# Routing of tokens inside an attention loop: fewer VectorE instructions, cut into short pieces, and a new schedule of the row scatters

## The reference, cut to what matters

```python
logits = jnp.einsum('btd,ed->bte', x, w_router)
probs = jax.nn.softmax(logits, axis=-1)
vals, idx = jax.lax.top_k(probs, TOP_K)
gates = jnp.sum(jax.nn.one_hot(idx, N_EXPERTS, dtype=x.dtype) * vals[..., None], axis=-2)
...
acc = acc + jnp.einsum('bted,bte->btd', y, gates)
```

## Time and profile before

| | |
|---|---|
| median of three runs | 961.9 us (958.61 to 963.03) |
| the profiled execution | 967.59 us, of which the span is 965.8 us |
| attention ends, on VectorE's last write of x | 486.3 us |
| TensorE busy in the span | 86% |
| mean granted TensorE clock | 0.919 of full speed |

### The profile page before, as it was taken

One profiled execution on the slowest core, in us unless ns is written; L12 is line 12 of the kernel. 1 busy time (PEld: TensorE's weight loads), 2 busy tenths in 40 slices (PEclk: granted clock), 3 DMA queues, 4 the chain that ended last, 5 costly groups with the idle time before them and its releaser, 6 DMA issues.

```text
span 965.8 us, 14197 instructions
## 1 busy us (share of the span) xinstructions
PE 832.7 (86%) x4630; PEld 454.8 (47%) x4630; DVE 731.3 (76%) x1571; ACT 633.4 (66%) x1119; POOL 469.4 (49%) x778
## 2 busy tenths in 40 slices
PE   5699999999988988798788799999974747899996
PEld 4123322223222222222176577877763425678884
DVE  6787888888898868983368588887767866787873
ACT  2157888888876777668467477776653682666773
POOL 3715273737355664536465048876576607411211
PEclk9569999999999989989679899999995877999999
DMA  7735546464636354303012346666616000000001
GB/s 243 164 113 164 125 147 143 141 149 136 153 125 156 98 170 87 146 16 112 20 63 101 116 165 225 249 214 216 210 58 235 17 17 1 1 0 13 12 22 44
DMA packets 45477, 110.72 MB, mean 115 GB/s; under 512 B 7886, under 2 KB 20814, under 8 KB 40086
## 3 DMA queue, kind: packets, MB, share of 16 engines
q1 hardware_dynamic: 39245, 97.86, 33.6%
q0 software_dynamic: 4992, 10.36, 3.1%
q10 hardware_dynamic: 1167, 1.60, 0.5%
HBM read 57.58 MB, written 51.03 MB: 112 GB/s over the span
## 4 chain that ended last, share of the span: by engine, by line
PE 48%; DVE 21%; ACT 10%; issue 9%; POOL 8%; DMA 3%; SPq 1%; another core or an unknown queue 0%; POOLq 0%; DVEq 0%; ACTq 0%
PE PS L1087 10%; DVE mx L895 9%; PE PS L1076 7%; PE PS L1057 4%; POOL yd L1303 4%; PE PS L320 3%; PE PS L322 3%; PE PS L321 3%; ACT E L801 3%; DMA HT<-xs 2%; PE PS L1039 2%; PE PS L1024 1%; DVE cb L2341 1%; ACT ov L807 1%; PE PS L2444 1%
## 5 line engine op out<-in xcount | busy, mean ns | idle before, releaser
L895 DVE TENSOR_REDUCE mx<-PS 128x2 f32<-128x1024 f32 x256 | 305.8, 1220 | 66.9 <-PE PS L1057 62.8
L801 ACT ACTIVATE E<-PS 128x512 f32<-128x512 f32 x512 | 274.3, 599 | 68.2 <-PE PS L1076 65.1
L1076 PE MATMUL PS<-Q,K 51*128 51x512 bf16 x512 | 168.0, 401 | 14.8 <-ACT E L801 10.6
L1057 PE MATMUL PS<-K,Q 48*128 48x512 bf16 x512 | 142.1, 411 | 27.5 <-DVE mx L895 26.6
L1087 PE MATMUL PS<-E,V 128*9 128x512 f32 x1024 | 142.0, 629 | 0.0
L1303 POOL DMA_INDIRECT yd<-yt,goes x92 | 99.4, 1080 | 45.9 <-issue 24.7
L1076 PEld LDWEIGHTS PS<-Q,K 51*128 51x128 bf16 x512 | 37.6, 95 | 165.7 <-ACT E L801 95.7
L1470 DVE TENSOR_TENSOR Gl<-Gf,Gh 128x512 fp32r<-128x512 f32 x117 | 84.6, 739 | 26.1 <-ACT Gh L1338 19.9
L513 POOL DMA_INDIRECT xs<-HT,pos x64 | 64.0, 1000 | 79.5 <-ACT E L801 45.6
L1332 ACT ACTIVATE Gf<-PS,WR 128x512 f32<-128x512 f32 x92 | 63.3, 689 | 42.6 <-PE PS L322 34.0
L2341 DVE SCALAR_TENSOR_TENSOR cb<-ye,gt,cb 128x128 f32<-128x128 f32 x224 | 60.3, 344 | 0.0
(11 more groups left out here) (418 smaller groups left out, 1854.9 us busy)
## 6 DMA issues: line engine op xcount, KB each, us to landing
WR<-wsd SPq DMA_DIRECT2D x23, 1028.0 KB
xs<-zero SPq DMA_DIRECT2D x8, 2112.0 KB, 7.3
wsd<-wsp SPq DMA_DIRECT2D x8, 1024.0 KB, 4.1
HT<-xs SPq DMA_DIRECT2D x23, 264.0 KB
dqk<-SPL SPq DMA_DIRECT2D x30, 192.0 KB, 2.8
Q<-dqk SPq DMA_DIRECT2D x14, 384.0 KB, 5.5
K<-dqk SPq DMA_DIRECT2D x14, 384.0 KB
stage<-in_w SPq DMA_DIRECT2D x9, 516.0 KB
```

The costliest lines, as they stand in the source:

```text
L801: e.activation(E[:, m % 4, n % 4], PS[:, bank["exp", n], :], ACT.Exp).then_inc(*k.inc("exp", n))
L895: e.tensor_reduce(mx[:, 2 * s % 96:2 * s % 96 + 2], PS[:, o:o + 2, :], AX.X, ALU.max, negate=True).then_inc(*k.inc("max", s))
L1057: return e.matmul(PS[:, o + n % 2, :], Q[r, b % 3, h // 2, qt * P:(qt + 1) * P], K[r, b % 3, h // 2, :], start=True, stop=True)
L1076: e.matmul(PS[:, o, :], K[r, b % 3, h // 2, kt * P:(kt + 1) * P], Q[r, b % 3, h // 2, :], start=True, stop=True).then_inc(*k.inc("exp_mm", n))
```

## The change

It fuses or drops ten VectorE instructions of each group of the routing (36 become 26): the copy of the best expert's index (`dve_one_hot` writes it to its place), the masking of the best before the second (one instruction for two), one copy in the gates, five of the starts (a masked scan, whose first column carries the count of the group before, replaces the corrections after it), and in the places the two multiplications and the two reductions become one of each, of double width. It cuts the parts into eleven pieces of two to four instructions, and moves them: group 0's best to batch 3 at i = 52 and 60, the rest to batch 4 at i = 4, 12, 22, 28, 34, 44, 48, 52, 60; group 1 likewise in batches 5 and 6; group 2 in batch 7 to i = 38, 48 and 54; group 3 in `ffn0` to (1, 3), (2, 1) and (2, 2), with `tiles_of` at (2, 3) in place of (3, 2). ScalarE's and TensorE's parts move with them; in `ffn0` `act_exp` goes from (2, 1) to (2, 0) and the ranks from (2, 2) to (2, 0). On GpSimd `wsplit` and `max_parts(b+1, 0)` go ahead of the scatters at 36. Two tiles more go in batch 7 at unit 58, tiles 22 and 23 behind the last product with V, and tiles 24 to 31 in `ffn0` without waits for gelus. On SyncE the load of the weights of tile 9 and of a pack of 1005 KB (`p2`) go behind the first three row loads. The core of the diff:

```diff
+        def dve_rest(e, k, M, wk):
+            k.wait_own("v")
+            e.scalar_tensor_tensor(wk[:, 3], wk[:, 0], -3.0e38, M, ALU.mult, ALU.add).then_inc(*k.inc("v"))
+            k.wait_own("v")
...
-            e.tensor_scalar(wk[:, 3], wk[:, 0], -3.0e38, None, ALU.mult).then_inc(*k.inc("v"))
-            k.wait_own("v")
-            e.tensor_tensor(wk[:, 3], wk[:, 3], M, ALU.add).then_inc(*k.inc("v"))
...
+        def dve_best_a(e, k, g):
             L, w, a, c = group(g)
             k.wait_ge("lgt", c // 4 - 1)
-            dve_top1(e, k, L, w)
-            k.wait_own("v")
-            e.tensor_copy(HT[:, a:c, 129], w[:, 4, :, 2])
+            dve_equal(e, k, L, w[:, 4, :, 0], w[:, 2])
+            dve_ordered(e, k, w[:, 2])
+
+        def dve_best_b(e, k, g):
+            L, w, a, c = group(g)
+            dve_one_hot(e, k, w[:, 2], HT[:, a:c, 129], w[:, 0])
+
+        def dve_second_a(e, k, g):
+            L, w, a, c = group(g)
+            dve_rest(e, k, L, w)
+            dve_equal(e, k, w[:, 3], w[:, 4, :, 1], w[:, 2])
+
+        def dve_second_b(e, k, g):
+            L, w, a, c = group(g)
+            dve_ordered(e, k, w[:, 2])
+            dve_one_hot(e, k, w[:, 2], w[:, 4, :, 2], w[:, 1])
...
-            chain(k, e.reciprocal(w[:, 4, :, 4], w[:, 4, :, 5]))
-            chain(k, e.tensor_tensor(w[:, 4, :, 5], w[:, 4, :, 3], w[:, 4, :, 4], ALU.mult))
-            e.tensor_copy(HT[:, a:c, 130], w[:, 4, :, 5])
-            e.tensor_tensor(HT[:, a:c, 131], w[:, 4, :, 4], w[:, 4, :, 5], ALU.subtract).then_inc(*k.inc("gates", g))
+            e.reciprocal(w[:, 4, :, 4], w[:, 4, :, 5]).then_inc(*k.inc("v"))
+
+        def dve_gates_b(e, k, g):
+
+            L, w, a, c = group(g)
+            k.wait_own("v")
+            chain(k, e.tensor_tensor(HT[:, a:c, 130], w[:, 4, :, 3], w[:, 4, :, 4], ALU.mult))
+            e.tensor_tensor(HT[:, a:c, 131], w[:, 4, :, 4], HT[:, a:c, 130], ALU.subtract).then_inc(*k.inc("gates", g))
...
-            chain(k, e.tensor_tensor_scan(inc, one[:, 0:8 * n], tot, 0.0, ALU.mult, ALU.add))
-            chain(k, e.tensor_copy(e8[:, 0, 1:8], over[:, 0:7, n - 1]))
-            e.tensor_tensor(cnt, over[:, :, n - 1], zero_, ALU.subtract)
-            chain(k, e.tensor_tensor(bs, base, zero_, ALU.subtract))
-            e.tensor_tensor(base, base, cnt, ALU.add)
-            chain(k, e.tensor_tensor(inc, inc, tot, ALU.subtract))
-            e.tensor_tensor(over, over, bs.unsqueeze(2).to_broadcast([P, 8, n]), ALU.add).then_inc(*k.inc("v"))
+            chain(k, e.tensor_tensor_scan(inc, mask(n), tot, 0.0, ALU.mult, ALU.add))
+            if g < 3:
+                e.tensor_copy(by_expert(starts(g + 1)[1])[:, :, 0], by_expert(inc)[:, :, n]).then_inc(*k.inc("v"))
...
-            for x in range(2):
-                chain(k, e.tensor_tensor(w[:, x], w[:, x], w[:, 3], ALU.mult))
-                chain(k, e.tensor_reduce(posf[:, x, a:c], w[:, x], AX.X, ALU.add))
+            e.tensor_tensor(w[:, 0:2], w[:, 0:2], w[:, 3:4].to_broadcast([P, 2, n, 8]), ALU.mult).then_inc(*k.inc("v"))
...
+            chain(k, e.tensor_reduce(posf[:, :, a:c], w[:, 0:2], AX.X, ALU.add))
...
@@ pool of attention: the loop over batches, and behind it
+                    wsplit(b + 1)
+                    if b + 1 < NB:
+                        max_parts(b + 1, 0)
                     if b >= 5:
                         paced(b, 36, SENT[b] + 4, SENT[b] + 6)
-                    wsplit(b + 1)
                     if b == 7:
                         paced(b, 48, SENT[b] + 6, SENT[b] + 8)
-                    if b + 1 < NB:
-                        max_parts(b + 1, 0)
+                        paced(b, 58, SENT[b] + 8, SENT[b] + 10)
...
-                scatter(e, k, 20, 22)
+                k.wait_ge("pv_mm", 16 * NB - 1)
+                scatter(e, k, 22, 24)
@@ act of attention
-                        if b in (4, 6) and i == 38:
+                        if b in (4, 6) and i == 30:
                             act_exp(e, k, b // 2 - 2)
-                        if b == NB - 1 and i == 46:
+                        if b == NB - 1 and i == 50:
                             act_exp(e, k, 2)
@@ pe of attention
-                        if b in (4, 6) and i == 46:
+                        if b in (4, 6) and i == 26:
                             pe_ranks(e, k, b // 2 - 2, bank_d(("rk", b // 2 - 2)))
-                        if b == NB - 1 and i == 54:
+                        if b == NB - 1 and i == 46:
                             pe_ranks(e, k, 2, bank_d(("rk", 2)))
@@ sp of ffn0
-                e.dma_start(stage[:].rearrange("p a n -> p (a n)")[:, 0:width(PACK2)], p2_d).then_inc(*k.dma("p2"))
                 k.wait_ge("ej")
-                for n in range(NS, NS + 3):
-                    load_w(n)
+                load_w(NS)
+                load_w(NS + 1)
                 k.wait_ge("scatter", NT - 1)
                 k.wait_ge("xt_mm", 2)
                 for n in range(NS, NS + 3):
                     load_x(n)
+                load_w(NS + 2)
+                e.dma_start(stage[:].rearrange("p a n -> p (a n)")[:, 0:width(PACK2)], p2_d).then_inc(*k.dma("p2"))
@@ pool of ffn0
-                for u, first in ((0, 22), (7, 24), (11, 26), (15, 28), (18, 30)):
-                    k.wait_ge("gelu", u)
-                    scatter(e, k, first, first + 2)
+                scatter(e, k, 24, NT)
```

141 lines of the change are left out of this document (84 added, 57 removed).

## The result

The changed kernel takes 925.86 us (median of four runs, 924.62 to 929.77) beside 961.27 us for the kernel before (four runs, 958.61 to 963.03). The ratio is 0.9636, with a 95% interval of 0.9613 to 0.9659: 3.6% faster. The profiled execution took 929.77 us, of which the span is 928.0, beside 967.59 and 965.8 before: 37.8 us less, where the sum of the prediction was 30.6.

The account below looks back on a forecast made before the run. TensorE was taken to bound attention, losing time to waits and the low clock behind them. Terms -6.4 + 0.5 - 4.2 - 7.0 - 7.0 - 6.5 = -30.6 us gave 937.0 profiled, 931.3 median; range 919 to 946.

Parts of the forecast that it names:

- The bound and the cover: Attention: TensorE sets the pace, VectorE has 7.2 us a batch to spare, the two-bank ring swallows about 0.8 us.
- Windows 3 and 5: Attention: best and second, 11 instructions or 3.1 us, move in and fit the spare time; +0.5 us for both.
- Batch 4: Attention: short pieces fit VectorE's spare time, leaving 3.0 of the lost 9.4 us; -6.4 us.
- Batch 5: Attention: GpSimd's new order removes the 1.11 us wait for the maxima's parts and the low clock behind; -4.2 us.
- Batch 6: Attention: the 2.82 us wait at the rank products and the low clock behind it mostly go; -7.0 us.
- Batch 7: End of attention: 7.6 us of ScalarE's exponentials to be had, less 0.6 for the last scatter; -7.0 us.
- `ffn0`: First feed-forward stage: scatters end 9.4 us earlier, removing TensorE's 6.55 us wait for tile 7's rows; -6.5 us.
- The term for the ranks: In `ffn0`: act_exp and the ranks at (2, 0) come late, close behind chosen, by up to 1 to 2 us.
- It does not do what it says: Rival, attention: GpSimd's long instructions cause the waits, not VectorE's burst length; 958 to 964 us, chance 0.05.
- The clock keeps falling: Rival, attention: short waits remain and keep lowering the clock, so the gain is 16.6 us: 945; chance 0.20.
- Slower: Rival, batches 4 to 6: the ring stays full and the lower clock holds throughout; 967 us and up, chance 0.04.
- The price of an instruction: VectorE routing: one less is worth 0.20 us or more by trace; ten fewer give 2.0 to 2.8 us a group.

Follow-up runs that it names:

- chips 13 and 6: The changed kernel run again, unedited, against the kernel before: 943.19 us, ratio 0.9739, on the first chip; 944.7 us, ratio 0.9702, on the second.
- the order alone: The kernel before, with only GpSimd's wsplit and max_parts moved ahead of the scatters of units 36 and 48: 961.05 us, ratio 0.9876.
- whole parts: The changed kernel with best to places of groups 0 and 1 back at the old places in batches 4 and 6, uncut: 944.75 us, ratio 0.9746.
- the bursts: The changed kernel with 3, 6 and 9 idle VectorE instructions in a row added in batches 1, 2 and 3, at i = 2 and 32: 948.98 us.

## Why the prediction was right, and where its steps were not

Forecast 931.3 us, range 919 to 946; measured 925.86. On chips 13 and 6 the change is worth 27.4 and 29.3 us for the 30.6 of the sum. Point by point, against the profiled execution's sum:

**The bound and the cover** were right. VectorE's 7.2 us to spare took the pieces, the ring swallows 0.87 us of a burst, and where bursts are kept long, waits of 1.08 us return; the longer ones there have an instruction in front of them that GpSimd held up.

**Windows 3 and 5**: +0.5 forecast for both; batch 3 alone paid 0.7, batch 5 can't be told from its spread.

**Batch 4**: -6.4 forecast, -5.3 measured. One idle of 1.32 us is left at 294.61, where I had said none over 1 us would be. It is not the length of the piece of i = 44: that piece's double-width multiplication took 2.42 us, and ended 0.2 us behind GpSimd's L741 (timelines of VectorE and GpSimd).

```profile
291.00 2.42 DVE L526 TENSOR_TENSOR wk<-wk 128x192 f32<-128x192 f32 x1
```

```profile
290.85 2.35 POOL L741 TENSOR_TENSOR wsp<-stage,wsp 128x1024 fp32r<-128x1024 f32 x1
```

So the new places met GpSimd's long instruction here. With all 36 instructions in pieces the batch is 53.1 us, and no gain of the smaller number can be told.

**Batch 5**: -4.2 forecast, -6.4 measured in the result's profiles. The wait of 1.11 for the parts and the low clock behind it were the right mechanism: undoing the order brings a wait of 1.08 us back, 6.6 us at 0.50, and 55.9 us of window, 4 to 5 over the changed kernel's 51.2 and 52.1. That the 2.6 us went too which I could put to no cause is shown by no run; with the order alone a gap that no engine explains takes a good part of the gain away again.

**Batch 6**: -7.0 forecast, -9.2 measured. The wait of 2.82 became 1.36 at the counts. In the two later profiles of the changed kernel the window is 51.6 and 51.8, so the gain is nearer 6 there. In front of the 2.82 stood the instruction of the earlier trace rows that GpSimd held up. So here too GpSimd's order has a share, which I gave it only in batch 5: without it the window is 54.2 us for 51.3, with one instruction held again.

**Batch 7**: -7.0 forecast, -9.3 measured, **and this is the step that failed**: "`act_exp` moves from i = 46 to 50 and `chosen` from 42 to 38: that is eight units, or 4.7 us, more room, against 3.79 missing". The room was not what was missing. `chosen` was late because the weights' split lay over two instructions of `best` ahead of it and held them for 3.5 us, and GpSimd's order takes it away; with the old places `act_exp` is still in time, with the old order the batch is as long as before. I had the pattern in hand, in batch 6, and didn't look for it in batch 7. The scatter of tiles 22 and 23, for which I took 0.6 us between 0 and 4, ends 0.3 us behind VectorE, and 0.7 and 1.4 in the two later profiles; with `places` at i = 56 it is the 4 of my upper end. I had written that the prediction is wrong if the end of attention is GpSimd's. It is GpSimd's, by so little that the time doesn't show it: the test should have been given with a size.

**`ffn0`**: -6.5 forecast, -9.9 in the first pair of profiles. I had the last scatter 9.4 us earlier in the stage: its last DMA ends 39.8 us after the end of attention, 5.1 earlier than the 44.9 of before. The term for the ranks, "1 to 2 us", measured 2.22. The wait for tile 7 went as said. But the run with `ffn0` as before puts only some 2.6 us of the stage on these edits, and the length of `ffn0` goes from 230.3 to 237 us over profiles of the same code, so that the size came near is partly luck.

**Left out of the sum**: 2.7 us more in the stages behind, and 1.4 less in the first two batches; the changed kernel's first batch starts its window at 119.5 to 120.3 us in its three profiles, 120.9 before, so that is chance.

**The rivals.** *It does not do what it says* named GpSimd's long instructions as the cause of the waits. The wait of 1.43 in batch 4, those of 1.08 with whole parts and the bursts show that length counts by itself, so it fails as a whole. But for batch 7 it had the cause, and the remedy was the order; and the longest waits of batches 4 and 6, in the kernel before and with whole parts, have a held instruction before them. It should have had more than 0.05 as part of the forecast. *The clock keeps falling* did not come: 0.97 or over in every batch of the profile after, and 0.92 at the lowest, in batch 7 of the third. *Slower* found nothing: no batch is at the lower clock throughout.

**The price of an instruction.** By the Trainium skill's "VectorE: DVE Perf Modes" (section "The TRN2 errata") the estimate was 0.07 us, by the rows it is 0.20. The fourth stage answers: there the masking of 32 elements took two instructions, 0.44 us from the first start to the start of what follows, and takes one now, 0.23. For a chain in which each instruction waits for the one before, the trace decides against that figure. Where two do not depend on each other it agrees: in the kernel before, L2318 and L2319 of the fourth stage, four elements each, start at 825.29 and 825.36. The brief idles of the Trainium skill's "TensorE: Matmul & The Clock Gate" (section "A second HAM failure mode: psum-queue depth-cycling") did not bring the clock down again and again in attention: idles of 0.41 us stand in the clean batches too, at 1.00.

What the runs leave open: why the changed kernel gains 3.6% in the result and 2.6 and 3.0% on chips 13 and 6, where it is 17 and 19 us slower than there and the kernel before 9 and 13. The windows put 7 and 9 us of the changed kernel's in batches 4 to 7, and 3 and 5 in `ffn0`.

## What to carry to other kernels

When a short instruction takes many times its usual length, ask first which instruction of another engine lies over it, and only then where it stands in its own queue: one edit of GpSimd's order, which touches no instruction of VectorE, gave 9 us in a batch whose 36 instructions stayed as they were. A burst beside a ring of two banks is free up to what the ring swallows (0.87 us here), and costs its full length beyond; so pieces of that size, with time to spare around them, are worth trying before a shorter routine. And measure a part's worth by its own window: in the whole of this kernel, parts worth 3 us drown.
